# A two-layer graph network, a linear-attention mixer and gated experts on one core: the second graph layer's dense tiles and mu placed beside the mixer's last FFN tiles

## The reference, cut to what matters

```python
def _mgcn_conv(x, edge_index, edge_type, rel, W_in, W_out, W_loop, b, n):
    m = x[src] * rel[edge_type]
    m = concatenate([m[:half] @ W_in, m[half:] @ W_out])
    norm = 1.0 / maximum(deg, 1.0)
    agg = segment_sum(m * norm[dst][:, None], dst, n)
    return tanh(agg + x @ W_loop + b)
h = x + res * _mgcn_conv(x, ..., rel1, W_in1, W_out1, W_loop1, b1)
h = h + res * _mgcn_conv(h, ..., rel2, W_in2, W_out2, W_loop2, b2)
g = h @ mu_w + mu_b
for i in range(4):                      # the mixer, 8 heads, linear attention
    x = x + linear_attn(layernorm(x), Wq[i], Wk[i], Wv[i], Wo[i], bo[i])
    x = x + (gelu(layernorm(x) @ W1[i] + b1[i]) @ W2[i] + b2[i])    # 256 -> 1024 -> 256
# experts: of the layer norm of (input + graph result + mixer result)
gates = top two of four, softmax over gW, renormalized
out = z + shared_mlp(z) + sum_e gates[e] * expert_e(z)
```

## Time and profile before

| | before |
|---|---|
| median of three runs | 2058.72 us (2057.43 to 2061.12) |
| the profiled execution, its own time | 2060.31 us |
| its span | 2058.6 us |
| granted TensorE clock, mean | 0.979 of full speed |
| PE / DVE / ACT / POOL busy | 91% / 61% / 33% / 65% |

### The profile page before, as it was taken

The page is one execution under the profiler, slowest core; times in us unless marked ns, Lnnn a source line. Parts: engine busy times, 40 slices in busy tenths (PEclk is TensorE's granted clock), DMA queues, the critical chain, the costliest instruction groups (busy, mean ns, idle before and its releaser), DMA issues.

```text
span 2058.6 us, 32009 instructions
## 1 busy us (share of the span) xinstructions
PE 1880.9 (91%) x10496; PEld 1566.3 (76%) x10496; DVE 1259.6 (61%) x3295; ACT 674.2 (33%) x1858; POOL 1339.0 (65%) x1342
## 2 busy tenths in 40 slices
PE   3989999998999999989999897788988999899999
PEld 1558888886788888678888785566877778778998
DVE  6775576556657556665655654487656556456666
ACT  5432344343234334422433341122112112133443
POOL 5777777777777777777777227777777777720000
PEclk9999999999999999999999999899999999999999
DMA  8677666667766666776667337766666666650001
GB/s 240 186 247 217 199 188 193 204 198 239 229 197 190 196 202 197 239 227 196 192 205 215 94 114 262 222 200 213 199 192 201 194 199 198 148 106 14 14 16 36
DMA packets 191812, 371.61 MB, mean 181 GB/s; under 512 B 36589, under 2 KB 123035, under 8 KB 191656
## 3 DMA queue, kind: packets, MB, share of 16 engines
q0 software_dynamic: 78624, 225.58, 38.1%
q1 hardware_dynamic: 92986, 128.48, 19.1%
q10 hardware_dynamic: 20046, 15.57, 2.7%
HBM read 305.39 MB, written 64.95 MB: 180 GB/s over the span
## 4 chain that ended last, share of the span: by engine, by line
PE 58%; POOL 16%; DVE 10%; issue 7%; DMA 6%; ACT 2%; DVEq 1%; ACTq 0%; SPq 0%
POOL xg L837 13%; PE ps_down L2417 11%; PE ps_hid L2408 10%; PE ps_seg L2294 10%; PE ps_kv L2327 4%; DMA xg<-h_rows,idx_tab 4%; POOL rg L817 3%; PE ps_x L2372 2%; PE ps_hid L2757 2%; DVE xg L968 2%; PE ps_kv L2711 2%; PE ps_down L2711 2%; PE ps_x L499 2%; PE ps_hid L499 2%; PE ps_hid L2347 1%
## 5 line engine op out<-in xcount | busy, mean ns | idle before, releaser
L2294 PE MATMUL ps_seg<-xg,hot 128*125 128x257 f32 x1664 | 444.4, 395 | 85.6 <-DVE xg L968 84.8
L837 POOL DMA_INDIRECT xg<-h_rows,idx_tab x416 | 431.9, 1038 | 134.3 <-issue 116.4
L837 POOL DMA_INDIRECT xg<-xn_rows,idx_tab x416 | 431.3, 1037 | 127.8 <-issue 121.9
L817 POOL DMA_INDIRECT rg<-relation_rows,idx_tab x416 | 425.4, 1023 | 129.5 <-issue 129.2
L2294 PEld LDWEIGHTS ps_seg<-xg,hot 128*125 128x125 f32 x1664 | 293.9, 191 | 161.9 <-DVE xg L968 87.6
L2408 PEld LDWEIGHTS ps_hid<-hT,wff 128*128 128x128 f32 x3200 | 384.1, 192 | 15.8 <-issue 6.8
L2408 PE MATMUL ps_hid<-hT,wff 128*128 128x125 f32 x3200 | 387.9, 275 | 1.6 <-ACT gT L1950 0.9
L968 DVE TENSOR_TENSOR xg<-xg,rg 128x512 f32<-128x512 f32 x416 | 286.0, 688 | 157.2 <-DMA xg<-h_rows,idx_tab 129.5
L1950 ACT ACTIVATE gT<-ps_hid,b1p 128x125 f32<-128x125 f32 x800 | 225.9, 366 | 471.0 <-PE ps_hid L2408 470.8
L2417 PE MATMUL ps_down<-wff,gT 128*125 128x256 f32 x1600 | 368.0, 384 | 0.0
L2417 PEld LDWEIGHTS ps_down<-wff,gT 128*125 128x125 f32 x1600 | 299.7, 191 | 43.6
(11 more groups left out here) (362 smaller groups left out, 2391.4 us busy)
## 6 DMA issues: line engine op xcount, KB each, us to landing
second_relation_rows<-rg SPq DMA_DIRECT2D x104, 512.0 KB, 4.0
rg<-second_relation_rows SPq DMA_DIRECT2D x104, 512.0 KB, 3.9
wff<-L_mix_W ACTq DMA_DIRECT2D x8, 1024.0 KB, 7.0
rg<-relation_rows,idx_tab POOLq DMA_INDIRECT x416, 3.5
xg<-xn_rows,idx_tab POOLq DMA_INDIRECT x416, 3.3
xg<-h_rows,idx_tab POOLq DMA_INDIRECT x416, 3.7
h_rows<-rg SPq DMA_DIRECT2D x25, 112.0 KB
xres<-x POOLq DMA_DIRECT2D x5, 560.0 KB, 8.6
```

What stands on the lines that cost most here:

```text
L817: pool.indirect_dma_start(rg[:, k, :], None, rel_d, bass.IndirectOffsetOnAxis(ap=idx_tab[:, step, 1:2], axis=0))\
L837: pool.indirect_dma_start(xg[:, k, 0:D], None, rows, bass.IndirectOffsetOnAxis(ap=idx_tab[:, step, 0:1], axis=0))\
L2294: ins = pe.matmul(ps_seg[u // UW % 2][0:T, 0:AW], hot[:, s % HOTS, :], xg[:, s % RING, :], start=s % WIN == 0, stop=s % WIN == WIN - 1)
```

## The change

The dense stage behind layer 3 is taken apart. Its pieces (25 tiles and the extra "rest" piece of the split tile, which is number 11 of 26) are numbered by `s`: ten half pieces stand in each group of layer 3, at hooks `aside(0)` to `aside(9)` between its FFN pieces, on TensorE, VectorE and ScalarE. Half piece 2k turns the sums and rows of piece k and multiplies mu for piece k-2, half piece 2k+1 multiplies piece k and turns the finished rows of k-1. What is left over at the end (five half pieces) stands between layer 3 and the experts, beside the last norm of group 0. A piece may be scaled only when the windows of edges up to its nodes have been added; a line of due nodes says when, and if the edge list breaks it or the split tile isn't 11 to 13, a flag set in the prologue sends all edges to the general loop, which now stands at the start of layer 3.

The `h` rows are loaded by ScalarE's queue, two transfers a tile, instead of SP; the weights of the experts by SP into the ring of relation rows once message 396 or so is through, instead of by GpSimd; mu's weights by ScalarE into the buffer of the attention's output weights. `add_x` waits for the group's mu sums. The last norms, logits and gates of groups 1 to 4 move into the loop of experts, each group over five steps: statistics, rows, five transposes with the logits behind, softmax and gates.

The tables give 24 steps of the second pass from before layer 3 to layer 3: 36 to 32 and 92 to 72 before it, 60, 60, 60, 60, 48 to 64, 64, 64, 64, 56 in it.

```diff
--- before.py
+++ after.py
...
-STEPS_JOINT = (14, 14, 14, 36)
-STEPS_GROUP = ((20, 28, 26, 26, 26), (20, 28, 26, 26, 26), (20, 26, 26, 26, 92), (60, 60, 60, 60, 48))
+STEPS_JOINT = (14, 14, 14, 32)
+STEPS_GROUP = ((20, 28, 26, 26, 26), (20, 28, 26, 26, 26), (20, 26, 26, 26, 72), (64, 64, 64, 64, 56))
 DENSE_LAYER, DENSE_GROUP = 2, 4
...
-            sp.wait_ge(s_tr, (L * NT + GT))
...
+            sp.wait_ge(s_msg, UNITS + (STEPS2 - 2 * RING + LAST_STEPS) // UNIT + RU + 1)
...
                 pool.wait_ge(s_xr, NG * L + gi + 1)
+                pool.wait_ge(s_emz, (gi + 1) * GT)
                 for rows in (slice(0, CUT), slice(CUT, T)):
...
                 upto(m["up1"])
+                aside(0)
                 upto(m["down0"])
+                aside(1)
                 b.add_ffn(0)
...
                 early()
+                aside(8)
+                if (lay, gi) == (L - 1, NG - 1):
+                    last_norm(0)
...
+            def sums_scaled(k):
...
+                need = windows_of(SPLITS[-1] if t < 0 else t)
+                assert edges.added() >= need, (k, edges.added(), need)
+                dve.wait_ge(s_acc, WINS * 2 + edges.adds + 3)
+                edges.scaled += 1
+                if k > 1:
+                    dve.wait_ge(s_dtr, SLOTS + NB + k - 1)
+                at, factor = (self_split.rest, norm[:, ds(self_split.rest_norm, 1)]) if t < 0 else                     (self_split.tile_sums(t), norm[:, t:t + 1])
+                dve.tensor_scalar(sums2[k % 2], at_tile(acc, at)[:, 0:D], factor, None, ALU.mult).then_inc(s_sc, 1)
+            def product_biased(k):
...
+                i, product = NB + k, ps_kv[0:T, 0:D]
+                if k == 0:
+                    dve.wait_ge(s_gw, GL * (4 * 16))
...
+                    rest_bias(i, product)
...
+                dve.wait_ge(s_dy, i + 3)
+                dve.tensor_tensor(loop_tanh[t % 2], product, at_tile(gb2, self_split.tile == t), ALU.add).then_inc(s_db, 1)
...
+            def rows_updated(k):
...
+                dve.wait_ge(s_dt, NT + t + 1)
+                h = qrow[:, t % GT, :]
+                dve.scalar_tensor_tensor(h, loop_tanh[t % 2], res_b[:, 0:1], h, ALU.mult, ALU.add).then_inc(s_hn, 1)
+            def mu_added(k):
...
+                dve.wait_ge(s_emu, t + 1)
+                dve.wait_ge(s_xf, (L - 1) * NT + t + 2)
+                dve.tensor_tensor(z_row(t), z_row(t), ps_kv[0:T, D:2 * D], ALU.add).then_inc(s_emz, 1)
+            def dense_beside(s):
+                k = s // 2
+                if s % 2 == 0:
+                    rows_updated(k - 1)
+                    mu_added(k - 2)
+                    sums_scaled(k + 1)
                 else:
-                    dense_and_last(dense_tile, lambda t: z_beside(t, update))
...
+            def last_stats(gi):
+                ed = Chain(dve, s_ed, gi * NORM_STEPS)
+                dve.wait_ge(s_er[gi], MOVED)
+                for j in range(GT):
+                    ed(dve.bn_stats(stat[:, j, :], z_row(gi * GT + j)))
+                ed.wait()
+                for j in range(GT):
+                    ed(dve.bn_aggr(mv[:, j, :], stat[:, j, :]))
+                ed.wait()
+                inv_sqrt(dve, ed, mv[:, :, 1], var[:, :], seed[:, :], rstd[:, :], tmp[:, :])
+            def last_rows(gi):
+                dve.wait_ge(s_ed, (gi + 1) * NORM_STEPS)
+                for j in range(GT):
+                    t = gi * GT + j
+                    dve.tensor_scalar(at_tile(acc, t)[:, 0:D], z_row(t), mv[:, j, 0:1], rstd[:, j:j + 1], ALU.subtract,
+                                      ALU.mult).then_inc(s_exh, 1)
...
-                            dense_head(1)
-                    iteration(lay, gi, *edges.stage(at_group[lay, gi]), early, sums_done, joint_rest)
-            dense(1)
+                    def aside(s):
+                        if lay == L - 1:
+                            dense_beside(gi * (2 * GT) + s)
+                    if (lay, gi) == (L - 1, 0):
+                        general(1)
+                        self_split.read()
+                        sums_scaled(0)
+                        gate_order()
+                    iteration(lay, gi, *edges.stage(at_group[lay, gi]), early, sums_done, joint_rest, aside)
+            behind = NG * (2 * GT)
...
-            shift_logits(1)
             dve.wait_ge(s_ew, 16 * LAST_LOADS)
             for s in range(1, NT + 2):
+                gi, j = last_part(s)
                 if s <= NT:
                     gated_rows(s - 1)
                 if s > 1:
                     add_experts(s - 2)
                 if s <= NT:
                     add_biases(s - 1)
-                if s in GATE_STEPS:
-                    gate_steps[GATE_STEPS.index(s) + 1](1)
+                if gi < NG:
+                    if j == 0:
+                        last_stats(gi)
+                    if j == 1:
+                        last_rows(gi)
+                    if j == 3:
+                        logits(gi)
+                        shift_logits(gi)
+                    if j == 4:
+                        softmax(gi)
+                        top_two(gi)
+                        gates(gi)
...
+            def rows_turned(k):
...
+                act.wait_ge(s_etr, t + 1)
+                if t > 1:
+                    act.wait_ge(s_emu, t - 1)
+                copy(hTa[:, t % 2, :, :].rearrange("p c t -> p (c t)"), ps_x2[:, 0:KC * T]).then_inc(s_eT, 1)
+                if t + GT < NT:
+                    load_h1(t + GT)
...
                 up(0, None)
+                aside(0)
                 up(1, "up0")
                 if is_first(gi):
                     b.turn_alone(3)
                     b.turn_alone(4)
+                aside(1)
                 b.down(0)
...
+            def turn_sums(k):
...
+                if k == 0:
+                    pe.wait_ge(s_hT, (L - 1) * NT + 4)
+                if has_tile(k - 2):
+                    pe.wait_ge(s_eT, tile_of_piece(k - 2) + 1)
+                if not has_tile(k - 2):
+                    pe.wait_ge(s_dT, NB + k + 1)
+                pe.wait_ge(s_sc, NB + k + 1)
+                turned = transpose_rows(pe, ps_x2[:, 0:KC * T], sums2[k % 2])
+                if t >= 0:
+                    h = t % GT
+                    pe.wait_ge(s_hx[h], (len(range(h, NT, AHEAD)) + t // GT + 1) * MOVED)
+                    turned = transpose_rows(pe, ps_x2[:, KC * T:2 * KC * T], qrow[:, h, :])
+                turned.then_inc(s_dtr, 1)
+            def sum_product(k, split_tile):
...
+                if k == 0:
+                    pe.wait_ge(s_gw, GL * (4 * 16))
+                    pe.wait_ge(s_xa, (L - 1) * NT + (GT + 1))
+                pe.wait_ge(s_dT, NB + k + 2)
+                pe.wait_ge(s_db, NB + k + 2)
+                if has_tile(k - 2):
+                    pe.wait_ge(s_emz, tile_of_piece(k - 2) + 1)
+                weights = (rest_rows(1),) if t < 0 else (half_rows(1, t, split_tile), loop_rows(1))
+                multiply(ps_kv[0:T, 0:D], lambda m: sum_columns[k % 2][:, m * T:(m + 1) * T], *weights).then_inc(s_dy, 1)
+            def turn_rows(k):
...
+                if k + 1 < NB:
+                    pe.wait_ge(s_dT, NB + k + 3)
+                pe.wait_ge(s_hn, NT + t + 1)
+                transpose_rows(pe, ps_x2[:, 0:KC * T], qrow[:, t % GT, :]).then_inc(s_etr, 1)
+            def mu_product(k):
...
+                pe.wait_ge(s_eT, t + 1)
+                pe.wait_ge(s_emz, t)
+                pe.wait_ge(s_db, NB + min(k + 1, NB - 1) + 3)
+                for c in range(KC):
+                    ins = pe.matmul(ps_kv[0:T, D:2 * D], hTa[:, t % 2, c, :], mu_w[:, c, :], start=c == 0, stop=c == KC - 1)
+                ins.then_inc(s_emu, 1)
+            def dense_beside(s, split_tile):
+                k = s // 2
+                if s % 2 == 0:
+                    turn_sums(k)
+                    mu_product(k - 2)
                 else:
-                    dense_and_last(dense_tile, mu_beside)
+                    sum_product(k, split_tile)
+                    turn_rows(k - 1)
...
+            behind = NG * (2 * GT)
+            turn_last(0)
+            turn_last(1)
+            dense_beside(behind, split_tile)
+            for j in range(2, GT):
+                turn_last(j)
+            dense_beside(behind + 1, split_tile)
+            last_logits(0)
+            pe.wait_ge(s_ew, 16 * LAST_LOADS)
+            pe.wait_ge(s_gel, L * (2 * NT) + 2)
+            shared_1(0)
+            dense_beside(behind + 2, split_tile)
+            experts_1(0)
+            dense_beside(behind + 3, split_tile)
+            dense_beside(behind + 4, split_tile)
             for s in range(1, NT + 2):
+                gi, j = last_part(s)
+                def turn(i):
+                    if gi < NG and j == 2:
+                        turn_last(gi * GT + i)
                 if s < NT:
                     shared_1(s)
+                if gi < NG and j == 3:
```

(6 more changed lines are left out.)

724 lines of the change are left out of this document (407 added, 317 removed).

## The result

The changed kernel took 2033.4 us in the median of four runs (2030.8 to 2034.2), the kernel before 2059.9 beside it, so 26.5 us or 1.3% less. The ratio on record is 0.9846, 95% interval 0.9822 to 0.9870; it is not the quotient of the two medians, which is 0.987. Measured once more among the experiments it was 0.9862 (0.9842 to 0.9883), and on a slower chip 0.9981 (0.9940 to 1.0022), where no gain can be told (experiment 5). Forecast were 2029 us, a range of 2000 to 2058, and a chance of 0.81 for faster. The profiled execution took 2034.2 us with a span of 2032.5 and a mean clock of 0.976.

What follows compares the result with a forecast made beforehand. Gathers were taken to bound the second pass through layer 3, TensorE the dense stage; -38 + 64 - 98 + 41 + 1 = -30 us on 2058.7 gave 2029 us, range 2000 to 2058.

Steps and rivals of the forecast that it cites:

- A: Layer 2's last group with the joint stage: 128 steps become 104, -38 us (bounds -49 and -32).
- I take 151, as the 104th sum ran some 150 us into this window: Layer 2's last group and joint stage: length taken as 151 us, from a range of 150 to 157, where 189.0 were measured.
- B: Layer 3 takes 24 more steps and 25 dense tiles: 446 us long, +64 us (bounds +52 to +92).
- 346.3 as it is: Layer 3: TensorE's existing busy time of 346.3 us carried over, with about 5 us off for slow clock.
- the 7 for the split number: Layer 3's start: VectorE reads the split number and tests for the unsorted case, 7 us of waiting.
- The rival of the asides that hold VectorE: Layer 3: some 50 dense places delay VectorE's messages; 30 us more leaves no gain, at worst 2079 us; chance 0.11.
- the rival of waits that aren't filled: Layer 3: TensorE's waits fall elsewhere than the dense pieces, +92 us there, 2057 us in all; chance 0.10.
- C: Dense stage behind layer 3 shrinks from 119.2 us to a tail of 21: -98 us (-105 to -89).
- D: Loop of experts takes the norms of groups 1 to 4: +41 us (bounds +14 and +61).
- The circle: Loop of experts: TensorE's and VectorE's work in series, 38.2 us per group where five tiles took 27.5.
- rival (3): Loop of experts: waits of about 5 us halve the clock, 5 us each in four groups, 20 us, so 2049; chance 0.08.
- E: Prologue: seven small VectorE operations, +1 us (0 to 1.4); last weights through SP cost 0.

Runs made afterwards that it cites:

- experiment 5: Changed kernel, unaltered and in two variants (Thin, fewer ahead), on two chips; unaltered: ratio 0.9981 on the slower chip, 0.9862 (2031.9 us) on the other.
- Thin: Changed kernel without three of four products per second-layer dense tile and one of two per mu tile: 2028.5 us, ratio 0.9845; slower chip 0.9939.
- fewer ahead: Changed kernel with 56 instead of 72 steps in layer 2's last group, 72, 72, 64, 64, 56 in layer 3: 2031.8 us, ratio 0.9867; slower chip 1.0015.
- Experiment 4: Changed kernel with the step tables of before (36 and 92 steps ahead of layer 3; 60, 60, 60, 60, 48 in it): 2047.1 us, ratio 0.9924.
- experiment 3: Changed kernel with 20 extra unread transposes on TensorE ahead of the first last-norm transpose of groups 1 to 4: 2024.8 us, ratio 0.9809.
- experiment 1: Changed kernel with each group's last norm, logits and gates spread over its five steps in the loop of experts: 2003.3 us, ratio 0.9698.

## Why the prediction was right, and where it wasn't

**What bounds which stretch** held. The gather queue bounded the second pass, the dense stage was TensorE's, and putting one beside the other hid most of it: in layer 3 the dense work cost 41.1 us with 24 steps more, the 98.2 of the tail are gone. Thin and fewer ahead show that layer 3 now stands at both limits, within 7 us of each other.

**A, -38 forecast, -27 measured.** The step that failed is "I take 151, as the 104th sum ran some 150 us into this window". In the kernel before that sum ran there because 92 steps stood in the group and the rest were strung along the joint stage. The steps of the joint stage are placed by its own chain, and that chain starts when the group ends. The runs show how little that chain shrinks: from the group's last FFN product to layer 3 it took 67.1 us before, with 36 steps, 60.9 with 32, and 62.9 in fewer ahead, again with 32. The group itself went from 121.9 to 101.1 us. So the 104th sum came at 162 us, not at 150. A step saved ahead was worth 1.1 us here and 1.3 in the next 16 (fewer ahead), not 1.58. The upper end of the term, -32, missed too.

**B, +64 forecast, +41 measured**, outside its bounds of +52 to +92. Most of it is TensorE's own work, 412.6 us busy for the 427 that I had. The step that failed is "346.3 as it is" with only 5 us off for the slow clock. Experiment 4 has it: the same steps with the dense pieces are 404.35 us busy, 58 more than before and not 70. The pieces aren't what was mis-sized. Line by line, the work that had been there already is counted some 16 us shorter (the edge sums 13.8, the other four lines together 2.0), which leaves 74 for the pieces, where 74.9 were forecast. Busy time of a TensorE that waits is not the same as that of one that doesn't. An estimate of where the 16 us lie: each of the 46 waits leaves a last record whose full 0.38 us are counted although the next could start after 0.22, 7 us in all; and the clock was at 0.50 for 17 us of layer 3 before and for 10 in experiment 4, which is 3 more (in the changed kernel it never is, which makes 8). That split is argued, and some 6 us of the 16 stay open. The rest of B's error is idle time, 10.2 us for the 12 + 7 that I set: the 7 for the split number don't show, the longest wait at the layer's start is one of 2.6 us for a message. The rival of the asides that hold VectorE is out: they wait 3.6 us in all. So is the rival of waits that aren't filled: 6.3 us of 34.9 are left.

**C, -98 forecast, -98.2 measured.** Its pieces were less exact than the sum: TensorE reached the first transpose of the last norm 2.3 us behind the last FFN product, not 4, and the clock was at 0.84 over the 21 us, which is 3 us lost for the 2 forecast.

**D, +41 forecast, +52 measured.** The circle was right in kind and place: TensorE's wait on the transpose of the last norm in the third tile, VectorE without a gap from late in the fifth through the first and second, periods of 37.6, 42.0, 40.0 and 42.0 us for the forecast 38.2. What was mis-sized is the clock, which the sum left out: with the waits filled (experiment 3) the periods are 37.5, 38.3, 39.9 and 38.3. I had put "whether 5 us do what 7.9 did no row shows" and gave rival (3) 0.08, expecting the waits to be split. They came in one piece of 4.7 to 4.9 us each, and at each the clock stood at 0.50 for 6.8 us. Two stretches of 3.4 us behind logits, with TensorE busy, come on top, which neither the sum nor a rival had; they make the second and fourth group 2 us longer than the third. That is 34 us of the loop in all. Sum and rival (3) were true at once, but the rival's price of 5 us a wait was too high: a stretch begins while TensorE still waits, and only 4.1 to 5.2 of its 6.8 us are work, so it costs 2.0 to 2.6 us, and all six together 12.7 (an estimate: half of the 25.4 us busy in them), against 11 missing in D. The row that the price came from says so too: 5.61 us busy in 10.00. The page that I cited (the Trainium skill, TensorE: Matmul & The Clock Gate, The HAM clock gate) agrees with these rows: the clock went down in waits of 4.7 us too, and came back after some work. Experiment 3 puts the part of the clock at the waits at 8 to 11 us, and experiment 1 the price of the whole order at 33.

**E, +1 forecast, +6 measured.** 5 us of it arose in layer 1 (370.0 to 375.0), of which the change touches nothing. On chips where the kernel before takes some 2060 all versions with other tables had 374.6 to 377.6 there, the one with the tables of before 369.1, although the tables differ only behind that layer. Why, no run here settles.

**Sizes beside the total.** That 2029 stood so near 2033 was luck in part: B's error carried A's, D's and E's. And the "own range" of 2012 to 2045 isn't what half of each term's bounds adds up to: that is 2000 to 2061. The range that I stated, 2000 to 2058, doesn't rest on it.

## What to carry to other kernels

When work is moved beside a stretch that waits, the busy time there grows by less than the added work (58 us for some 74 here), since the work around it no longer waits and is counted shorter; price the whole by the busy time of a full stretch and by the queue's floor, and take whichever is longer. When steps are taken out of a stage, ask which part of it has a chain of its own: the joint stage kept 61 to 63 of its 67 us, although the group in front of it got 21 and then 43 us shorter. When pieces are put into a tight loop on an in-order engine, look for the first instruction on the other engine that needs the last piece: moving the transposes behind three later blocks of TensorE's products gave 25 us in the loop with no work removed.
